# First layer of a two-layer graph network: weights ahead of the neighbour sum, and the first batch's scores in the setup program

## The reference, cut to what matters

```python
# x: (8, 1024, 256) float32; adj: (1024, 1024) of 0/1, 1 in 64 set
h = relu(layernorm(x))                                  # first layer
mi, mj = h @ W[:, :256].T, h @ W[:, 256:].T
deg = adj.sum(axis=1)
x = x + deg[:, None] * (mi + b) + adj @ mj
h = relu(layernorm(x))                                  # second layer, 4 heads and then 1 head
Wh = h @ W_head;  e = leaky(f1[i] + f2[j])              # f1, f2: Wh times two vectors a
attn = softmax(where(adj > 0, e, -1e9));  head = elu(attn @ Wh)
# the same once more on the concatenated heads with W_out, then
# ffn = relu(out @ w1 + b1) @ w2 + b2; x = x + layernorm(ffn + out) * gamma + beta
```

## Time and profile before

| | us |
|---|---|
| median of 3 runs (lowest, highest) | 1752.98 (1749.63, 1754.22) |
| the profiled execution's own time | 1755.2 |
| its span, first to last instruction | 1753.4 |
| busy in the span: PE, DVE, ACT, POOL | 1600.1, 1479.5, 1395.3, 1011.4 |
| setup program ends | 86.9 |
| first masked row of the main program | 101.2 |

### The profile page before, as it was taken

How to read it: one execution, slowest core, us unless ns; L and a number is a source line. 1 busy time by engine, 2 the same in 40 slices (tenths; PEclk the granted TensorE clock), 3 DMA queues, 4 the chain that set the end, 5 groups by cost and what they waited for, 6 DMA issues and landing times.

```text
span 1753.4 us, 36311 instructions
## 1 busy us (share of the span) xinstructions
PE 1600.1 (91%) x13224; PEld 1323.0 (75%) x13224; DVE 1479.5 (84%) x2524; ACT 1395.3 (80%) x1854; POOL 1011.4 (58%) x1414
## 2 busy tenths in 40 slices
PE   5539998999999999999999998999899998989875
PEld 3417887788778887888778887888777887878753
DVE  5965999879998899979998899979998897978573
ACT  4157899879978899878978898888987899789560
POOL 2054657647665666746666566845657465765261
PEclk9769999999999999999999999999999999999978
DMA  7054797759876796859966897858967599797462
GB/s 234 1 145 89 129 198 135 114 92 189 173 115 110 138 197 128 130 91 178 181 111 114 124 197 142 125 94 168 189 114 121 103 162 175 121 122 136 90 113 32
DMA packets 742866, 233.00 MB, mean 133 GB/s; under 512 B 708352, under 2 KB 736000, under 8 KB 742560
## 3 DMA queue, kind: packets, MB, share of 16 engines
q1 hardware_dynamic: 733728, 222.26, 70.2%
q0 software_dynamic: 8960, 8.42, 4.2%
HBM read 38.54 MB, written 16.94 MB: 32 GB/s over the span
## 4 chain that ended last, share of the span: by engine, by line
PE 49%; DVE 15%; ACT 11%; DMA 8%; issue 8%; SPq 3%; POOL 2%; ACTq 0%; DVEq 0%; POOLq 0%
PE ps L1194 12%; PE ps L1224 8%; PE ps L1218 8%; PE ps L1219 8%; PE ps L1238 4%; DVE p_lo L989 4%; PE ps L1251 4%; ACT xr L858 3%; DMA pt_lo<-p_lo 3%; PE ps L1316 3%; DVE xr L982 3%; DMA pt_hi<-p_hi 3%; ACT xr L864 2%; ACT p_hi L871 2%; PE ps L1318 1%
## 5 line engine op out<-in xcount | busy, mean ns | idle before, releaser
L1218 PE MATMUL ps<-pt_hi,hv_hi 128*128 128x256 f16 x2048 | 463.8, 274 | 1.2 <-DMA pt_hi<-p_hi 1.1
L1219 PE MATMUL ps<-pt_hi,hv_lo 128*128 128x256 f16 x2048 | 464.0, 274 | 0.0
L989 DVE SCALAR_TENSOR_TENSOR p_lo<-xr,rden,p_hi 128x1024 f16<-128x1024 f32 x320 | 409.9, 1282 | 50.0 <-ACT p_hi L871 28.9
L871 ACT ACTIVATE p_hi<-xr,rden 128x1024 f16<-128x1024 f32 x320 | 365.8, 1143 | 35.3 <-POOL rden L795 21.7
L864 ACT ACTIVATE xr<-xr,shift 128x1024 f32<-128x1024 f32 x320 | 365.4, 1142 | 1.9 <-POOL shift L808 1.8
L793 POOL TENSOR_SCALAR den<-sums 128x1 f32<-128x1 f32 x320 | 166.6, 521 | 303.6 <-ACT xr L864 300.7
L982 DVE CUSTOM_DVE_ANT_0 xr<-cat,mask_add 128x1024 f32<-128x1024 f32 x256 | 311.6, 1218 | 8.9 <-DMA cat<-f_rows 4.5
L858 ACT ACTIVATE xr<-xr,f1h 128x1024 f32<-128x1024 f32 x256 | 292.8, 1144 | 9.7 <-DVE mx L982 9.7
L806 POOL TENSOR_SCALAR zt<-mx,f1h 128x1 f32<-128x1 f32 x256 | 181.1, 707 | 181.0 <-DVE mx L982 170.8
L1224 PE MATMUL ps<-pt_lo,hv_hi 128*128 128x256 f16 x2048 | 266.7, 273 | 8.7 <-DMA pt_lo<-p_lo 8.7
L795 POOL TENSOR_TENSOR rden<-den,minus_one 128x1 f32<-128x1 f32 x320 | 245.7, 768 | 26.7
(11 more groups left out here) (195 smaller groups left out, 3150.8 us busy)
## 6 DMA issues: line engine op xcount, KB each, us to landing
cat<-f_rows SPq DMA_DIRECT2D x32, 512.0 KB, 4.6
out<-xx SPq DMA_DIRECT2D x32, 256.0 KB, 3.0
xx<-in_x SPq DMA_DIRECT2D x28, 256.0 KB, 3.2
out<-fin POOLq DMA_DIRECT2D x28, 256.0 KB, 4.6
pt_hi<-p_hi SPq DMA_TRANSPOSE x320, 3.3
pt_lo<-p_lo SPq DMA_TRANSPOSE x320, 3.3
adj_i<-in_adj SPq DMA_DIRECT2D x4, 1024.0 KB, 11.1
f2o<-f2o_rows SPq DMA_DIRECT2D x8, 512.0 KB, 4.7
```

The source lines that it names most:

```text
L871: nc.scalar.activation(p_hi[:, k % P_SLOTS, :], xr[:, k % X_SLOTS, :], ACT.Copy, scale=rden[:, k % 8:k % 8 + 1]).then_inc(hi_done, 1)
L989: nc.vector.scalar_tensor_tensor(p_lo[:, k % P_SLOTS, :], xr[:, k % X_SLOTS, :], rden[:, k % 8:k % 8 + 1], p_hi[:, k % P_SLOTS, :], ALU.mu ...
L1218: nc.tensor.matmul(to, vh, hi, start=t == 0, stop=False)
L1219: nc.tensor.matmul(to, vl, hi, start=False, stop=False)
```

## The change

1. **First layer.** The tokens h are split token-major, transposed by four DMAs per batch (`turn_h0`, new offsets `turn_h0_0`, `turn_h0_1`), and multiplied by both halves of W0 at once (`m0` to `m3`, two tiles of tokens each: six matmuls of 512 columns and one of 256 columns that adds b, per tile). ScalarE and VectorE split only the 128x512 neighbour half into `mj_hi`/`mj_lo`; VectorE adds degree times the own half to x directly. Then `x1` is the neighbour sum of mj: 128 matmuls of 256 columns. `z`, `d`, `cat_high`, `cat_low` and `add_bias` are gone.
2. **Setup program.** W0 and b are loaded ahead of the adjacency matrix; batch 0's first layer goes the same new way; squares for the norms are bfloat16; the scales of the four-head part are worked out apart from those of `W_out`. Batch 0's x is written out, its scores made, saved and loaded back broadcast at the end of the setup program.
3. **Order in the main program.** ScalarE does `g_high` and `ht_high` behind `rectify` and `high_part`; VectorE does `g_low` behind `masked_row`, and `ht_low` ahead of `low_part`; TensorE's `project` stands ahead of `attend` in a step. The offset tables have new numbers.

```diff
-            def z(s, k, c):
-                last = product(to[:, c * 512:(c + 1) * 512],
-                               [(h[:, jt, k * P:(k + 1) * P], adjT[:, jt, c * 512:(c + 1) * 512]) for jt in range(T) for h in (h0_hi, h0_lo)])
-            def d(s, k):
-                for t in range(T):
-                    last = product(to[:, t * P:(t + 1) * P], [(h[:, t, k * P:(k + 1) * P], diag_deg[:, t, :]) for h in (h0_hi, h0_lo)])
-            def x1(s, i):
-                pe.wait_ge(cat16_done, 4 * s)
-                for t in range(half):
-                    last = product(to[:, t * F:(t + 1) * F], [(cat16(a, k)[:, tok], w[:, k, :]) for k in (2, 0, 3, 1) for a, w in ((0, w0_hi), (0, w0_lo), (1, w0_hi))])
+            def tokens_by_w0(to, u):
+                for t in (2 * u, 2 * u + 1):
+                    both = to[:, t % 2 * 512:t % 2 * 512 + 2 * F]
+                    parts = [(h[:, k, t, :], w[:, k, :, :].rearrange("p c f -> p (c f)")) for k in range(KF) for h, w in ((h1_hi, w0_hi), (h1_hi, w0_lo), (h1_lo, w0_hi))]
+                    for i, (h, w) in enumerate(parts):
+                        nc.tensor.matmul(both, h, w, start=i == 0, stop=False)
+                    last = nc.tensor.matmul(both[:, 0:F], pick[:, :], b0_rows[:, :], start=False, stop=True)
+            def neighbours(to, i, t0, n):
+                for t in range(t0, t0 + n):
+                    tile = i * half + t
+                    last = product(to[:, t * F:(t + 1) * F], [(adjT[:, jt, tile * P:(tile + 1) * P], m[:, jt, :]) for jt in range(T) for m in (mj_hi, mj_lo)])
+            def m(s, u):
+                to, full = open_bank(f"m{u}", s)
+                pe.wait_ge(h0T_in[u // 2], 2 * (s + 1) * DMA)
+                last = tokens_by_w0(to, u)
+            def x1(s, i, c):
+                to, full = open_bank(f"x1_{i}", s)
+                pe.wait_ge(m_done, 4 * s)
+                last = neighbours(to, i, 2 * c, 2)
+            def turn_h0(s, i):
+                for (whole, part), ready in (((hs_hi, h0_hi), h0hi_half), ((hs_lo, h0_lo), h0_half)):
+                    sp.wait_ge(ready, 2 * (s - 1) + i + 1)
+                    sp.dma_start_transpose(whole[:, half_of]..., part[:, tiles, :]...).then_inc(h0T_in[i], DMA)
+            def mj_high(s, u):
+                nc.scalar.activation(mj_hi[:, 2 * u:2 * u + 2, :], ...[:, :, F:2 * F], ACT.Copy, scale=2.0 ** -M_LOG)
+            def m_low(s, u):
+                nc.vector.scalar_tensor_tensor(mj_lo[:, 2 * u:2 * u + 2, :], both[:, :, F:2 * F], 2.0 ** -M_LOG, mj_hi[...], ALU.mult, ALU.subtract)
+                for t in (2 * u, 2 * u + 1):
+                    last = nc.vector.scalar_tensor_tensor(xx[:, t, :], both[:, t % 2, 0:F], deg_sc[:, t:t + 1], xx[:, t, :], ALU.mult, ALU.add)
-        STEADY = dict(..., z00=-32, z01=-32, d0=-30, z10=-26, z11=-26, d1=-24, cat_high0=-31, ..., x1_0=-21, x1_1=-20, ...)
+        STEADY = dict(..., h0_low1=-34, turn_h0_0=-38, turn_h0_1=-34, m0=-31, m1=-30, m2=-29, m3=-28, mj_high0=-30, mj_high1=-29, mj_high2=-28, mj_high3=-27,
+                      mj_low0=-30, mj_low1=-29, mj_low2=-28, mj_low3=-25, x1_00=-24, x1_01=-23, x1_10=-22, x1_11=-22, ...)
-        SECOND = dict(..., h0_high1=-34, h0_low1=-32, z00=-31, z01=-29, d0=-29, z10=-28, ...)
+        SECOND = dict(..., h0_high1=-34, h0_low1=-34, turn_h0_0=-38, turn_h0_1=-35, m0=-33, m1=-33, m2=-32, m3=-32, ...)
-        CLOSING = dict(ff1_0=0, ff2_0=3, ff1_1=3, ff2_1=5, hidden_0=1, hidden_1=4, y_0=3, y_1=7, ...)
+        CLOSING = dict(ff1_0=-1, ff2_0=2, ff1_1=4, ff2_1=6, hidden_0=1, hidden_1=5, y_0=3, y_1=9, ...)
 # setup program, SP, after the last weight load
+                    for u in range(4):                    # batch 0's x is written out
+                        sp.wait_ge(x10_done, u // 2 + 1)
+                        ...
+                    for i in range(2):
+                        turn(LN_X1, hv_hi[0], hv_lo[0], i, h1T_in)
+                    sp.wait_ge(rows_done, 1)
+                    sp.dma_start(f2_rows[0:1, :, :]..., rows0[H:2 * H, :]).then_inc(f2_saved, DMA)
+                    sp.wait_ge(f2_saved, DMA)
+                    for m in range(H):
+                        load_row(sp, 0, m)
 # setup program, VectorE, its end
+                    low(LN_X1, hv_hi[0], hv_lo[0], 1)
+                    fold_out(0)
+                    fold_out(1)
+                    nc.vector.tensor_tensor(sqa[:, 16:32], wao_flat, wao_flat, ALU.mult).then_inc(sqa_done, 1)
+                    ...
 # setup program, TensorE, its end
+                    neighbours(psD, 1, 0, half).then_inc(x10_ps, 1)
+                    pe.wait_ge(sqa_done, 2)
+                    product(psA[:, 768:770], [(ones[:, :], sqa[:, 16 + 2 * k:18 + 2 * k]) for k in range(KH)]).then_inc(norm_ps, 1)
+                    pe.wait_ge(h1T_in, 4 * DMA)
+                    scores(psB).then_inc(rows0_ps, 1)
```

More of the change, by code:

```diff
@@ new lines, in scores_T @@
+            def scores_T(to, rows):
+                for t in range(T):
+                    last = nc.tensor.transpose(to[:, t * NF:(t + 1) * NF], rows[:, t * P:(t + 1) * P], ident[0:NF, 0:NF])
+                return last
+            return product, tokens_by_w0, neighbours, scores, scores_T
+        three = [(h1_hi, wh_hi), (h1_hi, wh_lo), (h1_lo, wh_hi)]
+        f1h = [sb(f"f1h{i}", [P, T, H], F32) for i in range(2)]
+        cat = sb("cat", [P, H, N], F32)
+        f2_rows = nc.dram_tensor("f2_rows", [B, H, N], F32).ap()
@@ L502, in _ @@
+                    last.then_inc(w0t_ps, 1)
+                    pe.wait_ge(sq0_done, 1)
+                    product(psC[:, 0:512], [(ones[:, :], sq0[:, k * 2 * F:(k + 1) * 2 * F]) for k in range(KF)]).then_inc(norm0_ps, 1)
                     for it in range(T):
@@ L1297, in f1T @@
                 pe.wait_ge(rows_done, s + 1)
-                for t in range(T):
-                    last = nc.tensor.transpose(to[:, t * NF:(t + 1) * NF], rows[:, t * P:(t + 1) * P], ident[0:NF, 0:NF])
-                last.then_inc(full, 1)
+                scores_T(to, rows).then_inc(full, 1)
             def ff1(p, i):
```

681 lines of the change are left out of this document (334 added, 347 removed).

## The result

The changed kernel takes 1759.61 us (median of 13 runs, 1756.68 to 1765.36); the kernel before took 1752.98 in the same comparison. The ratio is 1.0043 (95% interval 1.0032 to 1.0054): 0.4% slower, where 1.0% faster was forecast. The time lies 1.6 us above the end of the range.

What follows compares the result with a forecast made beforehand. TensorE was taken as the bound over most of a batch, ScalarE and VectorE close behind. Terms -6 + 7 - 4 - 10 - 4 = -17 from 1755.2 gave 1738, stated as 1736 us since that execution lay 2.2 above the median; range 1712 to 1758.

Steps and rivals of the forecast that it cites:

- TensorE's columns: TensorE's matmul time per batch falls from 26.1 to 25.2 us; over 7 batches of the main program, -6 us.
- The hand-off between the m's: Between m1 and m2 TensorE waits while psB is emptied: 1.0 us in 7 batches, +7 us (0 to +24).
- rival B: Slower by the psB hand-off: m2 costs 4.6 us if ScalarE reaches mj_high a row late; 1761 us, chance 0.15.
- The setup program: Main program starts at 90.2 instead of 86.9 us, first masked row at 102.7 instead of 101.2: +1.5 us (-3 to +7).
- The rule that it weighed: At the start, SP's DMAs are consumed in ring order, so x can't pass the row loads; otherwise row start 3 us earlier.
- The ramp: Batch 1's start: m0 to m3 ahead of the first attend, which starts at about 131 us; -4 us (-9 to +5).
- The four added transposes: SP's four more DMA transposes per batch find room at DMA share 0.74: 0 us (0 to +1 per batch).
- the 200 that was to show the forecast wrong: Sign in the steady batches: a period over 200 us (hand-off or DMA) means the forecast is wrong.
- 199 us or less: Sign in the windows of a batch: a period of 199 us or less would show the forecast right.
- The new order and offsets: Main program's steps: later ff1_1 gives -4 us (0 to -8), removed ht_lo waits give -10 us (-25 to +7).
- The likeliest sum: Whole kernel: the terms sum to -17 us, forecast 1736 us, 1.0% less; 1728 to 1743 had chance 0.42.

Runs made afterwards that it cites:

- E4: Changed kernel with the output head's score row saved in step -24, not -20, in every batch but the last: 1746.15 us, ratio 0.9967.
- E5: Changed kernel with the edits of E1, E2 and E4 together: 1732.25 us, ratio 0.9890 to the kernel before.
- E1: Changed kernel with batch 1's x1_10 and x1_11 issued in steps -22 and -21, not -18: 1747.26 us, ratio 0.9977.
- E2: Changed kernel with batch 1's m2 and m3 behind the first and second attend, first neighbour product a step later: 1746.63 us, ratio 0.9974.
- E8: Changed kernel with the steady batches' saves of x1 starting in step -17, not -21: 1748.25 us, ratio 0.9977.
- E13: Changed kernel, score row's save writing 4 KB in one piece (other values), not 1024 scattered words: 1733.73 us, ratio 0.9903.
- E3: Changed kernel with the three engines' order within a step as in the kernel before: 1773.21 us, ratio 1.0133.
- E11: E5 with the feed-forward stages (ff1, ff2, hidden, y) in the steps of the kernel before: 1743.62 us, ratio 0.9959.
- E7: Kernel before with only the new order of the three engines within a step: 1756.90 us, ratio 1.0032.
- E15: Kernel before with only the changed kernel's steps of the feed-forward stages: 1757.69 us, ratio 1.0043.
- E18: Kernel before with E13's edit, the score row's save in one piece (other values): 1739.44 us, ratio 0.9933.

## Why the prediction was wrong

**Right.** TensorE's columns, -0.87 per batch: over the three steady batches TensorE is busy 582.4 us in E4 and 583.8 in E5 after 585.0 in the kernel before, 0.4 to 0.9 less per batch where the clock is at 1.00. (The -5.9 us over the whole page agrees with the -6 by chance; it lies in the setup program.) The hand-off between the m's: 1.0 per batch, measured 0.87 (the row above has 11.8 us over 9 waits; 6.6 over 3 are in the ramp, 5.2 over 6 in the steady batches), so rival B, which named this wait for a slower kernel, did not happen. The setup program: 88.5 against 90.2, the first row 2.2 us earlier than forecast. The rule that it weighed, x behind the row loads, can be looked at now: the row loads were issued at 85.6, x at 88.6, and VectorE got x at 97.1; the sum's way gives 85.6 + 7.4 + 3.1 = 96.1, and x ahead of the rows would have come 3 us sooner than that.

**The first step that failed, "The ramp": -4, with the first attend at 131.** Up to unit 16 the gain is there (5.0 us), but the first `attend` came at 137.4. The step put the four m's "in time that was idle" and let the rows set the time of the first `attend`; it put no number on the emptying and none on the clock, though it had priced z of the kernel before at the lower one. The chain of the m's set the time: 25.3 us from 112.1 to 137.4, of it 6.6 in three waits of 2.2, and 18.7 of TensorE, 4.5 to 4.8 each and not the 2.8 of full clock (granted 0.69 to 0.76 from 112 to 137 us). At 2.8 each the same chain would have ended at 129.9 (my estimate: 112.1 + 11.2 + 6.6), so the clock is what the 131 lacks. Then the step argued that TensorE is full from 150 to 200 us and so the end of that stretch moves with its columns. It is full in the changed kernel too; what the argument left out is that a full TensorE lives from the stock of rows, and `x1_10`, `x1_11` and `x1_out1` in one step empty it (12.6 us of VectorE, then 5.5 us of TensorE). These three entries stand in the kernel's table; the step priced only m0 to m3. E1 and E2 give 11.6 and 12.1 us back, one by one, and unit 24 goes from 231.3 to 220.2 with both.

**The second, "The four added transposes": 0, by the DMA share.** No row shows harm from that DMA itself. But the prediction priced the queue by its share, and had no term for what the moved x1 and its moved saves would meet. The last product of the first layer now stands two steps sooner (-22, before -20), its saves three (-21, before -18). They are issued between the transposes in the step of the scattered save, which holds up what is issued beside it: ScalarE stands 9.2 us, ScalarE and VectorE lose work, and TensorE stands 30 us later. E4, E8 and E13 change this in three ways (13.3, 11.6, and 24.5 with the tail). The steady batch is 201.3 us in the changed kernel, past the 200 that was to show the forecast wrong; in E4 and E5 it is 198.4 and 198.8, which meets the "199 us or less", but in E8 and E13 200.3 and 199.7. So how much of the steady batches' loss is this stall stays open.

**"The new order and offsets": -10 and -4.** In the changed kernel the order is worth 15.8 us (E3) and the feed-forward places 12.1 (E11, measured in E5). The signs were right and both sizes too small, but that is luck: they were argued from waits of the kernel before, and there both cost, 5.6 and 7.5 us (E7, E15). The 10.4 us of ht_lo waits did go, for 16.0 us of g_lo waits. Why these places pay only beside the rest of the change I haven't isolated; it could be the new products or the new tables of the first layer.

The likeliest sum, 1736 us, is nearly that of E5, 1732.25: with three places in its tables moved, the change is worth about what was forecast. That the numbers meet is in part luck, since the order and the places of `ff1` measured 15.8 and 12.1 where the sum has 10 and 4. That the three places are the whole loss rests on E5 and this sum alone.

## What to carry to other kernels

Where a schedule is a table of steps, price each moved entry by what stands in its new step: who produces its input in that very step, and which DMA is issued there. Price a product at the clock that TensorE has at that place. A full bottleneck engine shows nothing while its suppliers stand still; look at their busy time in the same window, and at the bottleneck later (here 30 us). The total of a wait is not its cost: with 7.5 us of waits for transposes E3 was the slowest, with 59.6 E5 the fastest. Judge such a change with its tables fitted: places that gain 12 to 16 us in one version cost 6 to 8 in the other.

## What the runs showed of the hardware

A save of 1024 scattered words of four bytes (4 KB) holds up SP's transposes beside it: one issued 0.3 us before the save took 13.27 us in the chain of waits, where 3.3 us is usual, and with the same 4 KB in one piece ScalarE's waits for transposes fell from 64.0 to 21.7 us. The kernel before has it too: the transposes issued 0.1 us ahead of the save took 10.9 to 13.1 us in six of its batches, and 3.2 to 4.7 at the same place in E18. It doesn't happen each time: of the changed kernel's six high-part transposes 0.3 to 0.4 us ahead of the save, four took 12.1 to 13.8 us, two 3.2 and 5.1. The 13.27 us are made of signals that come one after another, from 588.4 to 593.8, beside the save's own (588.2 to 593.5). From its issue to the load that waits for it the scattered save takes 9.4 us (1648.32 to 1657.71 in the kernel before), in one piece 2.0 (1640.87 to 1642.87 in E13). The Trainium skill ("DMA: Bandwidth & Descriptors", section "Queues, rings and completion order") says that a completion signal is written only after every earlier write of the same DMA engine, across its queues. The row agrees as far as a slow write of one queue delays the signals of another; the transpose was issued before the save, so whether it is the signal or the data that waited no run here shows.
